# A quad's last three sampling slots are carried into the next quad, and slot operations are placed between products

## The reference

```python
x = x + _L0_conv_ref(_gn(x), ...)   # 4-bit activations, sign weights, 3x3 convolution, affine, ReLU
x = x + _L1_conv_ref(_gn(x), ...)
# inside the second layer
xf = jnp.fft.rfft2(x, axes=(2, 3))              # 56 x 29 frequencies
amp, pha = jnp.abs(xf), jnp.angle(xf)
amp3 = deform_conv(amp, wp_a, bp_a, wc_a)       # 3x3 deformable convolution
amp1 = conv2d(amp, w1_a, 0) + b1_a
pha3 = deform_conv(pha, wp_p, bp_p, wc_p)
pha1 = conv2d(pha, w1_p, 0) + b1_p
out_c = amp1*exp(i*pha3) + amp3*exp(i*pha1)     # written with sin, cos and small constants
xr = jnp.abs(jnp.fft.irfft2(out_c, s=(H, W), axes=(2, 3)))
return conv2d(xr, w0, 2) + b0                   # 5x5
```

## Time and profile before

| what | value |
|---|---|
| median of three runs | 7875.68 us |
| profiled execution, its own time | 7877.08 us |
| its span, first to last instruction | 7874.9 us |
| mean granted clock of TensorE, share of full | 0.862 |
| PE, DVE, ACT, POOL busy | 74%, 61%, 35%, 67% |
| chain that ended last | PE 49%, DVE 19%, POOL 12%, issue 10%, ACT 7% |

### The profile page before, as it was taken

The page is one execution under the profiler, slowest core; times in us unless marked ns, Lnnn a source line. Parts: engine busy times, 40 slices in busy tenths (PEclk is TensorE's granted clock), DMA queues, the critical chain, the costliest instruction groups (busy, mean ns, idle before and its releaser), DMA issues.

```text
span 7874.9 us, 106214 instructions
## 1 busy us (share of the span) xinstructions
PE 5804.1 (74%) x33682; PEld 2822.3 (36%) x33682; DVE 4787.2 (61%) x7421; ACT 2756.2 (35%) x5357; POOL 5285.3 (67%) x5044
## 2 busy tenths in 40 slices
PE   3577776878677876788768887687867787676765
PEld 2333333334333433334333433333433343233323
DVE  3366656576566765666655666557656676565641
ACT  2333333334233343334323343333423334232322
POOL 0277767777577766777667776777757776677760
PEclk7789888889888898889888898888988889888887
DMA  2222222222322223222222222222232222312120
GB/s 85 64 71 62 63 72 68 65 82 63 94 60 64 74 71 81 62 72 67 74 72 65 81 64 74 67 66 82 63 93 61 64 74 71 81 50 68 51 66 21
DMA packets 424838, 540.91 MB, mean 69 GB/s; under 512 B 310746, under 2 KB 318974, under 8 KB 417646
## 3 DMA queue, kind: packets, MB, share of 16 engines
q0 software_dynamic: 161280, 330.62, 16.0%
q1 hardware_dynamic: 262980, 203.17, 10.0%
HBM read 404.04 MB, written 116.94 MB: 66 GB/s over the span
## 4 chain that ended last, share of the span: by engine, by line
PE 49%; DVE 19%; POOL 12%; issue 10%; ACT 7%; DMA 2%; DVEq 1%; SPq 0%; ACTq 0%; POOLq 0%
PE pair L1049 21%; POOL gath L626 12%; PE ring L987 5%; PE ring L906 4%; PE ps_acc L1023 4%; ACT u L1081 3%; DVE gath L1625 3%; PE ps_def L1070 3%; DVE prod L1613 2%; ACT prod L1281 2%; DVE gath L1630 2%; PE ring L951 1%; PE ring L868 1%; PE ring L852 1%; DVE u L1435 1%
## 5 line engine op out<-in xcount | busy, mean ns | idle before, releaser
L626 POOL DMA_INDIRECT gath<-table_d,idx_all x5040 | 5285.1, 1049 | 2359.1 <-issue 1788.4
L1049 PE MATMUL pair<-clamp_x,tab 128*128 128x392 f32 (+1 forms) x5760 | 2830.7, 604 | 1183.5 <-DVE prod L1613 1176.2
L1613 DVE SCALAR_TENSOR_TENSOR prod<-prod,pair 128x392 f32<-128x392 f32 (+1 forms) x2880 | 1610.6, 570 | 1570.4 <-PE pair L1049 1494.8
L1281 ACT ACTIVATE prod<-ps_y,y_bias 128x392 f32<-128x392 f32 (+1 forms) x2880 | 1481.0, 597 | 2457.0 <-PE ps_acc L1023 2154.9
L1049 PEld LDWEIGHTS pair<-clamp_x,tab 128*128 128x128 f32 x5760 | 1142.5, 220 | 2487.9 <-DVE prod L1613 1751.1
L1625 DVE TENSOR_TENSOR gath<-gath,wgt 128x1152 f32<-128x1152 f32 x560 | 758.9, 1355 | 681.4 <-DMA gath<-table_d,idx_all 674.8
L1081 ACT ACTIVATE u<-ring 128x448 f32<-128x448 f32 (+7 forms) x1376 | 605.2, 479 | 877.1 <-PE ring L894 229.9
L1023 PE MATMUL ps_acc<-prod,w_samp 128*32 128x392 f32 (+1 forms) x5760 | 648.5, 523 | 6.5 <-DVE prod L1613 6.5
L1070 PE MATMUL ps_def<-xt,w_samp 32*32 32x224 f32 x5760 | 324.9, 380 | 223.7 <-DVE xt L1637 223.7
L987 PE MATMUL ring<-u,w 128*32 128x392 f32 x5120 | 457.0, 514 | 22.6 <-ACT u L1081 22.6
L906 PE MATMUL ring<-u,w_off 128*64 128x448 f32 (+1 forms) x2048 | 425.4, 514 | 26.4 <-ACT u L1081 26.4
(11 more groups left out here) (155 smaller groups left out, 4093.0 us busy)
## 6 DMA issues: line engine op xcount, KB each, us to landing
gath<-table_d,idx_all POOLq DMA_INDIRECT x5040
table_d<-u SPq DMA_DIRECT2D x192, 210.0 KB
point_d<-u SPq DMA_DIRECT2D x32, 406.0 KB
u<-point_d SPq DMA_DIRECT2D x32, 406.0 KB
u<-in_x SPq DMA_DIRECT2D x8, 1568.0 KB, 7.4
x_d<-u SPq DMA_DIRECT2D x8, 1568.0 KB, 5.8
xg_d<-u SPq DMA_DIRECT2D x8, 1568.0 KB, 5.3
u<-xg_d SPq DMA_DIRECT2D x32, 392.0 KB
```

Source lines behind the costliest of these rows:

```text
L626: pool.indirect_dma_start(gath[:, k % BUFS, n * CELL:(n + 1) * CELL], None, table_d[:, :], bass.IndirectOffsetOnAxis(idx_all[:, k, n:n + 1 ...
L1049: nc.tensor.matmul(bank[:, 0:size], tab[:, b * NB + br, j * 128:(j + 1) * 128], clamp_x[:, s % 2, 0:size], start=True, stop=True)\
L1281: nc.scalar.activation(prod[:, s % 2, j, 0:size], ps_y[:, 0:size], ACT.Relu, bias=y_bias[:, j:j + 1]).then_inc(relu_ready, 1)
L1613: v.scalar_tensor_tensor(rows, rows, 1.0, bank[:, 0:size], ALU.min, ALU.mult)\
```

## The change

`CARRY` = 3. A walk with a front now does slots 0 to 66 only. A walk with a back begins with the rest of the quad before: after unit 1 comes slot -3, after unit 3 slot -2, after unit 5 slot -1, after unit 6 the last sum, its put and the store, and only then the first piece. `KEEP` is gone: slots follow PE's cost evenly over the whole list, the last stage included. The loop variable becomes `old`, the quad before, so that the carried entries can name it. In DVE's program a slot is a generator now: `slot` only puts it into the list `woven`, and the next unit takes one of its four steps after each product. What is left is done at the end of that unit, or before the next slot, sum, put or the end of the walk.

```diff
--- before.py
+++ after.py
@@ -118,7 +118,7 @@
             ("back1", 0), ("back1", 1), ("back1", 2), ("back1", 3)]
 UNIT, SLOT, SUM = (44, 29), (0, 31), (50, 4)
 
-KEEP = 66
+CARRY = 3
 
 
 def pieces(name, step):
@@ -135,6 +135,7 @@
     for n, s, _ in steps + last:
         pe, ve = pe + sum(p[0] for p in pieces(n, s)), ve + sum(p[1] for p in pieces(n, s))
     out, at = [], {"pe": 0, "ve": 0, "unit": 0, "slot": 0, "sum": 0, "put": 0}
+    slots = NK - CARRY if has_front else NK
 
     def add(kind, n, cost):
         out.append((kind, n))
@@ -159,16 +160,21 @@
             at["put"] += 1
 
     def fill(share):
-        while at["pe"] + at["ve"] < share * (pe + ve) and at["unit"] + at["slot"] < SUNITS + NK:
-            if at["unit"] == SUNITS or at["slot"] < pace * at["pe"] / pe:
+        while at["pe"] + at["ve"] < ahead_by + share * (pe + ve - ahead_by) and at["unit"] + at["slot"] < SUNITS + slots:
+            if at["unit"] == SUNITS or at["slot"] < slots * (at["pe"] - pe_by) / (pe - pe_by):
                 slot()
             else:
                 unit()
 
-    whole = sum(p[2] for n, s, _ in steps for p in pieces(n, s))
-    rest = sum(p[2] for n, s, _ in last for p in pieces(n, s))
-    pe_last = sum(p[0] for n, s, _ in last for p in pieces(n, s))
-    pace = KEEP * pe / (pe - pe_last) if last else NK
+    if has_back:
+        for k in range(-CARRY, 0):
+            unit()
+            unit()
+            out.append(("slot", k))
+        unit()
+        out += [("sum", -1), ("put", -1), ("store", -1)]
+    ahead_by, pe_by = at["pe"] + at["ve"], at["pe"]
+    whole = sum(p[2] for n, s, _ in steps + last for p in pieces(n, s))
     done = 0
     for name, step, ahead in steps + last:
         if name == "load":
@@ -178,14 +184,18 @@
             out.append(("piece", (name, step, ahead, i)))
             at["pe"], at["ve"] = at["pe"] + p[0], at["ve"] + p[1]
             done += p[2]
-            if at["slot"] < NK:
-                fill(done / (whole + rest))
-    while at["slot"] < NK or at["unit"] < SUNITS:
-        slot() if at["slot"] < NK else unit()
-    if at["sum"] < NK // SETS:
-        add("sum", at["sum"], SUM)
-    add("put", at["put"], SUM)
-    out.append(("store", 0))
+            fill(done / whole)
+    while at["slot"] < slots or at["unit"] < SUNITS:
+        slot() if at["slot"] < slots else unit()
+    if has_front:
+        assert at["sum"] == NK // SETS - 1
+        if at["put"] < at["sum"]:
+            add("put", at["put"], SUM)
+    else:
+        if at["sum"] < NK // SETS:
+            add("sum", at["sum"], SUM)
+        add("put", at["put"], SUM)
+        out.append(("store", 0))
     return out
 
 
@@ -204,7 +214,7 @@
             work += UNIT[0]
         elif kind == "sum":
             work += SUM[0]
-        elif kind == "slot":
+        elif kind == "slot" and n >= 0:
             slots.append(work)
         elif kind == "piece":
             cost = pieces(n[0], n[1])[n[3]][0]
@@ -218,7 +228,9 @@
 
 def gather_pace(has_back, has_front):
 
-    events, slots, _ = pe_events(has_back, has_front)
+    events, slots, work = pe_events(has_back, has_front)
+    assert CARRY <= LEAD
+    slots.append(work)
     pace = []
     for k in range(LEAD, NK):
         lo, hi = slots[k - LEAD], slots[k - LEAD + 1]
@@ -548,7 +560,7 @@
         FZ, FO, FT, FD = 0, KWG, KWG + OFILLS, KWG + 2 * OFILLS
         BY, BA, BZ, BO = 0, NG // 2, NG, 0
 
-        def walk(q, has_back, has_front, stage, unit, slot, products, put, store):
+        def walk(q, old, has_back, has_front, stage, unit, slot, products, put, store, end):
 
 
             done = PROLOGUE_FILLS
@@ -565,28 +577,30 @@
                 elif kind == "unit":
                     unit(q, n)
                 elif kind == "slot":
-                    slot(q, n)
+                    slot(q, n) if n >= 0 else slot(old, NK + n)
                 elif kind == "sum":
-                    products(q, n)
+                    products(q, n) if n >= 0 else products(old, NK // SETS - 1)
                 elif kind == "put":
-                    put(q, n)
+                    put(q, n) if n >= 0 else put(old, NK // SETS - 1)
                 else:
-                    store(q)
+                    store(q if n >= 0 else old)
+            end()
 
         def nothing(q, n=0):
             pass
 
-        def program(eng, stage, unit=nothing, slot=nothing, products=nothing, put=nothing, store=nothing):
+        def program(eng, stage, unit=nothing, slot=nothing, products=nothing, put=nothing, store=nothing,
+                    end=lambda: None):
 
             done = 0
             for name, step in PROLOGUE:
                 for _ in stage(name, 0, step, stage_no(-1, name), done // 2):
                     pass
                 done += fills(name, step)
-            walk(0, False, True, stage, unit, slot, products, put, store)
-            with eng.Fori(1, NQ - 1) as q:
-                walk(q, True, True, stage, unit, slot, products, put, store)
-            walk(NQ - 1, True, False, stage, unit, slot, products, put, store)
+            walk(0, None, False, True, stage, unit, slot, products, put, store, end)
+            with eng.Fori(0, NQ - 2) as old:
+                walk(old + 1, old, True, True, stage, unit, slot, products, put, store, end)
+            walk(NQ - 1, NQ - 2, True, False, stage, unit, slot, products, put, store, end)
             done += quad_fills(False, True) + (NQ - 2) * quad_fills(True, True)
             done += quad_fills(True, False)
             for name, step in EPILOGUE:
@@ -1601,6 +1615,18 @@
                 v.tensor_scalar(clamp_x[:, s % 2, 0:size], ps_x[:, 0:size], 0.0, 1.0, ALU.max, ALU.min)\
                     .then_inc(clamp_ready, 1)
 
+
+
+            woven = []
+
+            def step():
+                if woven and next(woven[0], True):
+                    woven.pop()
+
+            def finish(q=0, n=0):
+                while woven:
+                    step()
+
             def unit(f, s):
                 base = f * QUAD_USES + unit_uses(s)
                 size = part(s)
@@ -1614,8 +1640,14 @@
                         .then_inc(pair_free[j % 2], 1)
                     if j == 1 and s + 1 < SUNITS:
                         clamps(f, s + 1)
+                    step()
+                finish()
 
             def slot(q, here):
+                finish()
+                woven.append(slot_steps(q, here))
+
+            def slot_steps(q, here):
                 k = q * NK + here
                 buf = here % BUFS
 
@@ -1624,12 +1656,15 @@
                 rows = gath[:, buf, :].rearrange("p (n c) -> p n c", c=C)
                 v.tensor_tensor(rows, rows, weights.unsqueeze(2).broadcast_to([128, 4 * TAPS, C]), ALU.mult)\
                     .then_inc(weighted, 1)
+                yield
                 corner = gath[:, buf, :].rearrange("p (n k c) -> p n (k c)", n=TAPS, c=C)
                 low, high = corner[:, :, 0:2 * C], corner[:, :, 2 * C:]
                 dve.wait_ge(weighted, 3 * k + 1)
                 v.tensor_tensor(low, low, high, ALU.add).then_inc(weighted, 1)
+                yield
                 dve.wait_ge(weighted, 3 * k + 2)
                 v.tensor_tensor(high[:, :, 0:C], low[:, :, 0:C], low[:, :, C:], ALU.add).then_inc(weighted, 1)
+                yield
                 dve.wait_ge(weighted, 3 * k + 3)
                 if here % SETS == 0:
                     wait(dve, def_full, q * (NK // SETS) + here // SETS)
@@ -1645,7 +1681,7 @@
                 v.transpose(deform[:, n * SETS:(n + 1) * SETS, :].rearrange("p k c -> p (k c)"),
                             ps_def[:, 0:SETS * 32]).then_inc(def_ready, 1)
 
-            program(dve, stage, unit=unit, slot=slot, put=put)
+            program(dve, stage, unit=unit, slot=slot, products=finish, put=put, end=finish)
 
 
 def constants():
```

## The result

The changed kernel takes 7749.06 us (median of four runs, 7737.97 to 7764.76), the kernel before beside it 7876.3: a ratio of 0.9842, 95% interval 0.983 to 0.9854. That is 127 us less. I had forecast 60 less, 7816, with a range from 7715.

What follows compares the result with a forecast made beforehand. The prediction held that waits, different in different places, bound the kernel, no engine being busy over 74%. Boundaries -139, middle quads +54, weave +28 and quad 7 -3 made -60 us: 7816 us, 8-in-10 range 7715 to 7905.

Steps and rivals of the forecast that it cites:

- The end of a walk: From a quad's last unit to the next first product: 66.5 us becomes 34.6, 31.9 less, 23.2 net per boundary.
- What moves into the units: Three carried slots cost 5.1 us and the sum 4.6 among the next walk's first units; one slot less ahead, -1.0.
- Redistribution: Seven units moved from mid-list to the front lose 9 us per middle quad, bounds 0 and 29.5.
- the carry: The change without the weave, over boundaries, middle quads and quad 7: -139 + 54 - 3 = -88 us.
- The weave: Slot operations between DVE's products: +4 us for each of quads 0 to 6, bounds -32 and +32.
- slots without fills beside them: Weaving some 19 such slots of a quad saves 0.6 us each and a bit more: -15 us per quad.
- the third rival: PE waits 2.7 us at the head of each sum, so the kernel turns slower, 7915 us; chance 0.14.
- Slots beside fills: Some 20 to 25 woven slots begin after the first product, delaying the fourth pair up to 0.25 us: +5.
- Quad 7: Later gathers cost 11 us, shrinking pace waits give 14: net -3 with boundary 6-7, bounds -35 and +11.
- The rule of the Trainium skill: Two-port VectorE operations lock GpSimd's descriptor port: gathers beside units 0.1 us longer, quad 7 about 4 us later; not summed.
- The gain is whole: Rival: the weave gains more than it costs, removed units are worth their full 4.22 us: 7688 us; chance 0.15.
- the gathers take the gain: Rival: stretches at POOL's pace spread to half of a middle quad, total 7874 us; chance 0.16.

Runs made afterwards that it cites:

- e1: The changed kernel with each slot done as one block on DVE again, so the carry alone with nothing between products: 7677.52 us.
- e7: The kernel before with only seven of a walk's 90 units moved to its head, nothing carried and nothing woven: 7861.62 us.
- e9: The changed kernel with only each seventh slot, which a sum follows, woven between products and the others as blocks: 7742.58 us.
- e10: The changed kernel with only each seventh slot as a block and the other six of a set woven between products: 7717.4 us.
- e13: e4 with each of a slot's four operations put ahead of a product, not behind it: 7498.64 us.
- e4: The changed kernel without POOL's waits for PE's progress in the last five slots of a walk: 7684.38 us.
- e12: The changed kernel with slots as blocks, no POOL waits for PE's progress in a walk's last five slots, and two carried slots for three: 7682.62 us.

## Why the prediction came out as it did

- **The end of a walk, right in kind and nearly in size.** 34.6 us forecast for quad 1, 37.4 measured; 29.8 us saved in the mean for the 31.9 forecast. The extra is the last gathers: they landed at 2074.5, 29.2 us after the last unit, for the 28.7 of the earlier trace rows, and "issue" of 2.58 us ahead of the clamp.
- **What moves into the units, right.** I had 9.7 us for three slots and the sum (8.7 with the slot that is missing before the last unit). From unit 0's first product to unit 7's it is 38.3 us in e1 and 38.8 in the changed kernel, for the 29.8 of seven bare units in e7: 8.5 and 9.0.
- **Redistribution, the step that failed.** I took +9 per middle quad and had 0 as the lower bound. In e1 the stretch from unit 7's first product to the last unit takes 827.2 us, where all the units took 867.8 before. Seven units and a slot less explain 30.8 of these 40.6, so the value is about -10: 19 us per walk below my term, and over six walks as much as the whole error of the carry (199 for my 88). e7, with the units moved alone, shows +3.6. So the gain comes only with the rest of the carry's order; which part of it brings the gain no run separates. I counted only where a unit stands in another's shadow, and gave the denser middle no credit.
- **The clock, which I didn't price.** In the kernels with blocks the products of a walk amount to the same work if those at 0.50 are halved: 720.5 - 154.6/2 = 643.2 before, 705.1 - 122.3/2 = 643.9 in e1, 643.0 to 644.8 in the others. So e1's PE is busy 15.4 us less per walk for the clock alone, about 14 of them outside the boundary, and stands 16.6 less (214.3 to 197.7). That is most of the 19 us above. Quad 0 goes the same way: in e1 PE is busy 610.7 us in it for 629.6, with 130.0 us at 0.50 for 165.1; in the changed kernel, 12.5 us below its forecast there, 624.0. The changed kernel doesn't have this gain: 152.1 us of a walk are at 0.50 for 154.6, and the same sum is 648.8, 5 us more, which I can't explain. There the clock explains nothing of the 15 us per walk by which I was low; PE stands 29.4 us less. I had seen the clock at 0.50 behind the 28-us wait, put its price at one slow sum, and not asked what the other waits cost.
- **The weave, wrong in two terms.** I had +4 per quad, +28, with bounds of -32 and +32 per quad. It is +7.1 per walk and +15.5 for the end, 72 us in the runs. The sums were not the fault: I had +14 per quad for them, and e9 measures +9.5 per walk, the clock behind them included, with a wait of 1.8 us for my 2.7. The other two terms together, -15 for slots without fills beside them and +5 for the fourth pair, are what e10 weaves: +1.0 for -10. PE does stand 15.5 us less there, so the saving was real, but it is busy for 16.5 more at the lower clock. The second term is quad 7, where I charged the weave nothing. So of the third rival the place was right, but not the size: 10 us per quad (72 over seven), under its +13, and against a carry twice as large as I had.
- **Slots beside fills, a step with the right sign and the wrong size.** "Now it begins after the first product" is in my text, at 0.25 us for some 20 to 25 slots. e13 undoes this, together with the transpose's place, and is 186 us faster than e4. In the slot shown, the work woven behind the product loses the fills as cover: the product waits for the fills, and so does the slot.
- **Quad 7, a term built on a misreading.** I took 833.7 - 787 = 46 us for pace waits and let them shrink by 14. There were none: POOL stood 192.0 us, all of it issue, and the 46 us are gathers longer than 0.94. The one row that decides it, POOL's group in that stretch, I hadn't read. The same holds in the middle, where I called POOL's idle time "mostly pace": of its 271 us in quad 2, 189 are the 0.30 us of 630 gathers. In quad 7 the gathers got slower, not denser: +12.4 us. With the later start (+11.1, forecast 11) that is +23.5; the end is 21.6 longer, where I had -3.
- **The rule of the Trainium skill** (SBUF — State Buffer, "Who interferes with whom") points the right way, and I had it at +4 us for quad 7 and left it out of the sum. Measured in the changed kernel's trace: gathers that start beside DVE's additions of two SBUF inputs (`gath<-gath`) take 1.27 us in the mean (551 of them), for 0.98 (507) before, those beside nothing 0.94 and 0.95. Beside the long multiply, which has two SBUF inputs as well, they take 1.35 us (562) and took 1.33 (524) before, so the trace of before did say which operation disturbs a gather.
- **The other rivals.** "The gain is whole" is what the carry did (7678 for its 7688), but with a weave that cost where this rival has it gain. Of "the gathers take the gain" only quad 7's part came.
- **What the marks said.** Walks shorter by over 20 us were to mean that the weave gains. They are 25 us shorter and the weave costs: the mark read two terms as one. The errors of the sum had opposite signs, 199 us for the carry's 88 and 72 for the weave's 28, so 44 us of the first one's 111 were hidden by the second. That the result still fell into the range is owed to this and not to the mechanism.

## What to carry to other kernels

Work that is moved behind the start of a unit loses the cover of whatever that start waits for: put it ahead of the wait, and let only what is short follow between (e13; its rows show it for one slot). Price each wait of PE by its length and by what the clock does behind it: busy time with the same products, divided between the two clock levels, tells how much of a difference is clock. An order that makes PE stand less can leave it at the lower clock for longer, as e10 and e12 did, so read both. And before calling a surplus over an ideal "waits", ask for the engine's own idle time in that stretch; it can be longer instructions.
